# A selective-scan recurrence on four engines: the first half of delta and dx, and the output projection with the residual, moved to other iterations

## What is computed

```
x = resid * rsqrt(mean(resid * resid) + EPS) * norm_w
skip = x @ skip_w.T
x = silu(causal_conv(x @ in_w.T, conv_w, 4 taps) + conv_b)
delta = softplus(x @ Wd1.T @ Wd2_w.T + Wd2_b)
Bm, Cm = x @ WB.T, x @ WC.T
h_l = exp(delta_l * A) * h_(l-1) + (delta_l * x_l) * B_l      # 512 channels x 16 states
y_l = sum over the states of h_l * C_l
y = (y + x * W_D) * silu(skip)
x = layernorm(resid + (resid + y @ out_w.T))
```

## Time and profile before

| | |
|---|---|
| median of 3 runs | 1925.93 us (1924.54 to 1927.51) |
| the profiled execution | 1923.67 us |
| its span, first to last instruction | 1921.8 us |
| busy: PE, DVE, ACT, POOL | 1619.1, 1483.1, 1084.0, 1258.2 us |
| largest group: the scans into ps_h, L690 | 160 x 2287 ns, 24.6 us of waits for ACT |
| mean granted TensorE clock | 0.939 |

### The profile page before, as it was taken

One profiled execution on the slowest core, in us unless ns is written; L12 is line 12 of the kernel. 1 busy time (PEld: TensorE's weight loads), 2 busy tenths in 40 slices (PEclk: granted clock), 3 DMA queues, 4 the chain that ended last, 5 costly groups with the idle time before them and its releaser, 6 DMA issues. The chain is left out here.

```text
span 1921.8 us, 32746 instructions
## 1 busy us (share of the span) xinstructions
PE 1619.1 (84%) x9596; PEld 1040.7 (54%) x9597; DVE 1483.1 (77%) x2444; ACT 1084.0 (56%) x2436; POOL 1258.2 (65%) x936
## 2 busy tenths in 40 slices
PE   7787877778787778874579999898899999999996
PEld 5454444445444444442246666665677555555685
DVE  5799899999999999999868887887633444444488
ACT  4777777788778777875324444444422333333325
POOL 1988888899888889988655788884320333333300
PEclk9889899999999998997679999998999999999999
DMA  7545555444545544446246765443156222222272
GB/s 222 138 102 129 114 133 124 99 106 103 122 110 133 133 111 108 97 106 147 64 117 161 185 184 154 134 138 95 54 170 231 86 85 85 85 86 85 71 268 88
DMA packets 179286, 238.30 MB, mean 124 GB/s; under 512 B 24714, under 2 KB 115725, under 8 KB 177070
## 3 DMA queue, kind: packets, MB, share of 16 engines
q1 hardware_dynamic: 160606, 200.64, 40.8%
q0 software_dynamic: 9888, 27.80, 4.1%
q10 hardware_dynamic: 8656, 8.18, 1.6%
HBM read 172.15 MB, written 65.90 MB: 124 GB/s over the span
## 5 line engine op out<-in xcount | busy, mean ns | idle before, releaser
L690 DVE TENSOR_TENSOR_SCAN ps_h<-ps_h,inject 128x1024 f32<-128x1024 f32 x160 | 365.9, 2287 | 24.6 <-ACT ps_h L534 24.6
L364 POOL TENSOR_TENSOR inject<-common,bc_n 128x2048 f32<-128x2048 f32 x63 | 285.7, 4548 | 86.1 <-issue 72.3
L364 POOL TENSOR_TENSOR inject<-dx_n,bc_n 128x2048 f32<-128x2048 f32 x64 | 290.2, 4547 | 0.0
L1518 ACT ACTIVATE expT<-ps_t 128x512 f32<-128x512 f32 x256 | 148.7, 596 | 199.2 <-PE ps_t L2015 195.2
L534 ACT ACTIVATE ps_h<-delta_n,a_neg 128x256 f32<-128x256 f32 x512 | 213.0, 462 | 61.8 <-DVE hc L703 42.4
L534 ACT ACTIVATE ps_h<-common,a_neg 128x256 f32<-128x256 f32 x512 | 212.0, 463 | 43.0 <-DVE hc L703 33.1
L1646 DVE TENSOR_REDUCE neg_max<-ps_s 128x2 f32<-128x512 f32 x256 | 172.8, 681 | 79.0 <-PE ps_s L2004 74.1
L373 POOL TENSOR_TENSOR h_pool<-h_pool,bc_n 128x1024 f32<-128x1024 f32 x96 | 226.8, 2363 | 0.0
L690 DVE TENSOR_TENSOR_SCAN h_pool<-ps_h,inject 128x1024 f32<-128x1024 f32 x96 | 218.6, 2277 | 5.7 <-ACT ps_h L534 3.0
L2666 PE MATMUL ps_uh<-arena,s_xT 128*128 x440 | 210.3, 601 | 4.9 <-issue 4.9
L2370 POOL DMA_INDIRECT token_results<-common,e_y_row x82 | 80.0, 976 | 188.7 <-DVE common L2519 188.7
(11 more groups left out here) (338 smaller groups left out, 3580.6 us busy)
## 6 DMA issues: line engine op xcount, KB each, us to landing
common<-dup_rows SPq DMA_DIRECT2D x120, 256.0 KB, 6.0
bc_n<-bc_rows SPq DMA_DIRECT2D x64, 256.0 KB, 4.4
delta_n<-dup_rows SPq DMA_DIRECT2D x64, 256.0 KB, 4.4
dx_n<-dup_rows SPq DMA_DIRECT2D x64, 256.0 KB, 7.5
arena<-slot_rows SPq DMA_DIRECT2D x110, 136.0 KB, 2.1
arena<-token_results SPq DMA_DIRECT2D x8, 1536.0 KB, 18.5
dup_rows<-delta SPq DMA_DIRECT2D x32, 256.0 KB, 4.0
dup_rows<-dx SPq DMA_DIRECT2D x32, 256.0 KB, 4.2
```

The lines of the kernel that those rows point to most:

```text
L364: nc.gpsimd.tensor_tensor(inject[:, at:at + 2, :, :], dx_n[c // 2][:, None, :, c % 2, :].to_broadcast([P, 2, JB, L]), bc_n[b % 2][:, 0, nq ...
L690: nc.vector.tensor_tensor_scan(out.rearrange("p j t -> p (j t)"), ps_h[k % 2][:, :, :].rearrange("p j t -> p (j t)"), inject[:, k % RING, ...
L1518: nc.scalar.activation(expT[:, h % (2 * HG), :, :], ps_t[h % 2][:, :, :], ACT.Exp).then_inc(h_exp, 1)
```

## The change

No instruction is added or removed. Four things move.
- ScalarE: the copy of the first half of delta stands ahead of the second half's logarithm in iteration 8, instead of behind it.
- VectorE: the first half of dx is made in iteration 8 instead of 9. Since iteration 8 is one that GpSimd weighs, it stands right behind scan 8.
- TensorE: the output projection is in iteration 2 instead of 3, and ahead of that iteration's sums.
- VectorE: residual and row statistics both stand in iteration 4 (before: 5 and 6), mean in 5 (7), variance in 6 (8). The later row steps stay.

```
@@ ScalarE's loop @@
+                if front and i == 8:
+                    take_delta(b + 1, 0)
                 if front and i in (6, 8):
                     softplus_log(b + 1, (i - 6) // 2)
                 if tail and i == 7:
                     layernorm_root(b - 1)
-                if front and i in (8, 10):
-                    take_delta(b + 1, (i - 8) // 2)
+                if front and i == 10:
+                    take_delta(b + 1, 1)
@@ VectorE @@
-            rows = (residual, row_stats, row_mean, row_var, None, square_root, newton, row_scale, row_shift)
+            rows = {4: (residual, row_stats), 5: (row_mean,), 6: (row_var,), 10: (square_root,), 11: (newton,),
+                    12: (row_scale,), 13: (row_shift,)}
...
-                if b > 0 and 5 <= i < 14 and rows[i - 5] is not None:
-                    rows[i - 5](b - 1)
-                if b < B - 1 and i in (9, 11):
-                    make_dx(b + 1, (i - 9) // 2)
+                if b > 0:
+                    for step in rows.get(i, ()):
+                        step(b - 1)
+                if b < B - 1 and i in (8, 11):
+                    make_dx(b + 1, i // 11)
@@ TensorE's loop @@
+                if tail and i == 2:
+                    project_out(b - 1)
                 sums(b, i)
...
-                if tail and i == 3:
-                    project_out(b - 1)
```

More of the change, by code:

```diff
@@ L811, in _ @@
                 split(q_rows[n], q_parts[n], 18 + 4 * (AHEAD + n), qk.q_split)
-            for step in rows:
-                if step is not None:
+            for steps in rows.values():
+                for step in steps:
                     step(B - 1)
```

## The result

| | before | after |
|---|---|---|
| median | 1925.24 us (4 runs) | 1948.06 us (1945.99 to 1953.10, 4 runs) |
| ratio | | 1.0125, 95% interval 1.0104 to 1.0146 |
| the profiled execution, its span | 1923.67, 1921.8 us | 1948.89, 1947.1 us |
| VectorE's period, dx to dx of the first half, mean of 14 | 55.49 us | 57.02 us |
| start of the phase after the recurrence (the cast to `ident_bf` on VectorE) | 951.80 us | 974.1 us |

The change makes the kernel 22.8 us slower, where I had forecast about 12 us (1938) and a range up to 1944. Of the 25.2 us between the two profiled executions 22.3 lie ahead of the phase that follows the recurrence. The direction and the place (the wait for delta ahead of dx) were as forecast; the size was not, since the wait has a second cause that I had left out.

The account below looks back on a forecast made before the run. VectorE's 55.25 us period was taken as the bound, nearly level with a loop through GpSimd. Batch 0's 1.76 us plus 14 x 0.77 gave 12.5, taken as 12.0: 1938 us, own range 1932 to 1944, 1925 to 1944 with B.

Parts of the forecast that it names:

- Batch 0: First batch, without residual: dx would come at 87.00 and scan 10 at 91.07 against 89.31, +1.76 us.
- The hole of the Silu session: VectorE ahead of scan 5: residual and statistics fill the 1.31 us hole, scan 5 stays, 1.25 us leave the path behind.
- The projection ahead of the sums: TensorE: projection runs 343.9 to 347.6, pushed-back sums are done by about 349.1, before their buffers are wanted, so free.
- dx ahead of scan 9: VectorE idles from scan 8's end to dx, 3.1 us instead of 1.13, with scan 9 queued behind; +0.77 us per batch.
- The loop over GpSimd gets slack: GpSimd restarts sooner after dx, TensorE's 1.49 us wait for it goes, db comes earlier; the loop gets 2.5 us of slack.
- delta copy at + 1.59 = 364.16: ScalarE: the delta copy ends at 364.16, directly after decay 10 at 362.57; dx then follows at 364.77.
- The sum: Whole run: 1.76 + 14 x 0.77 = 12.5 us slower, less 0.8 us of old longer waits, taken as 12.0.
- allowance of 0.4 us per batch: Upper range for an unseen later sum or copy collision, from the smallest margin, a 0.38 us hole; gives 1944 us.
- A: Rival: faster, the GpSimd loop sets the period and its ScalarE part shortens 1.70 us; 14 x 1.70 = 24, 1902 us; 5%.
- B: Rival: no change, ScalarE reaches decay 10 when scan 8 ends, needing 0.9 us saved between weighing 7 and delta; 1926 us; 10%.
- C: Rival: slower still, projection ends after 348.3 and the residual holds the scan; 1.25 us more per batch, 1955.5 us; 10%.
- The two holes that I named: GpSimd: about 4 us ahead of the new batch's injects (5.31 before), and a new hole for scan 9 ahead of injects 14 and 15.

Follow-up runs that it names:

- part 1 alone: Changed kernel with delta copy and dx put back as before, keeping the moved projection, residual and row steps: 1921.25 us, ratio 0.9990 to the kernel before.

## Why the prediction was right and wrong

- *Batch 0.* Right, nearly: from scan 5 to the first dx it is 19.32 instead of 20.86 us, and to scan 10 23.40 instead of 21.47, 1.93 us more where I had 1.76.
- *The hole of the Silu session.* Right: residual and statistics went into it without a wait ahead of them, 1.39 us from start to start of scan 5, and scan 5 did not move. The step from residual to statistics was 0.71 us, as taken from the row of the residual. By the rule of the Trainium skill (VectorE: DVE Perf Modes, "The DRAIN you can't avoid") that the semaphore costs nothing extra, as I had applied it, it would have been 0.59; here the measurement decides.
- *The projection ahead of the sums.* Right that it is free: nobody waited for it or for the sums behind it, and with part 1 alone the kernel is not slower. It isn't free wherever VectorE is sooner: with dx back in 9 the residual waited for it 5 times, 2.1 us in all.
- *dx ahead of scan 9.* Right, and the whole of the loss hangs on it: with dx back in 9 the same kernel is 1.0% faster than before. The wait that I worked out, 3.13 us, and the period, 56.02, are what the kernel shows where TensorE is kept at its full clock (3.12 and 56.01), and within 0.1 us in every third batch of the changed kernel.
- *The loop over GpSimd gets slack.* Right: ScalarE copied db at 357.55, with no wait, ahead of decay 7.
- *The step that failed* is "delta copy at + 1.59 = 364.16", right behind decay 10. The copy also waits for TensorE's sum of softplus (`take_delta` waits for `f_sp`, L501). I costed that sum nowhere. Before, it ended at 363.3 and the copy was due at 366.85, so it had 3.5 us of cover. In the changed kernel, in the batch shown, the copy was due at 370.61 and the sum began at 365.32; at the full clock it would have ended at 369.02, with 1.6 us of cover left. So the copy's move alone would not have made it late. But the change also stretched TensorE's idle time ahead of the sum from 2.1 to 3.9 us, mainly by letting db come sooner (with db sooner and nothing else it is 3.6 us), and the sum ran at the lower clock and took 5.2 to 6.7 us instead of 3.7. Less the cover of 1.6, that is 0 to 1.4 us too late, and the copy waited 0 to 1.5 us. Against the kernel kept at the full clock it is 0.94 us a batch on the mean (57.02 against 56.08), 13.2 us in all.
- *The sum.* From scan 5 of batch 0 to the last scan 10 that stands behind a first-half dx, the profiled execution takes 23.3 us longer than before. My terms give 12.5 us. Of the 3.4 us by which the old batches were longer than 14 x 55.25 all went, where I had taken 0.8 (and 12.5 - 0.8 is 11.7, not the 12.0 that I took). That leaves 9.1; batch 0 adds 0.2, the first period, with the longer scaling of `bq`, 0.8, and the sum of softplus 13.2: together 23.3 us. So the forecast was out by one large term that it didn't have, and the allowance of 0.4 us per batch was far too small for it.
- *What I read past.* The kernel before already had such matmuls at the lower clock (means of 731 to 810 ns in the same three groups, against 592), hidden under that cover.
- *The rivals.* A (faster, 1902) did not come. With dx left in 9 the kernel does get to 1907 us, but not at A's price: its 14 periods are 12.2 us shorter, where A had 14 x 1.70 = 24. B (no change) needed ScalarE to save 0.9 us ahead of the copy; it saved nothing, and no wait ahead of dx was under 3.2 us. C (the projection late) did not occur in the change. My upper end of 0.4 us per batch was taken from a margin among VectorE's and ScalarE's rows, and so could not hold a term from TensorE.
- *GpSimd.* The two holes that I named are there: the restart waits 4.3 us for the DMA on the mean (60.0 us in 14), where I had 4, and the injects wait for a scan of VectorE's 38.8 us in 15, 2.6 us each, where I had put a hole without a size.

## What to carry to other kernels

Move a producer's step sooner by all means, but leave its consumer, on an in-order engine, behind work that is ready: one scan and one weighing in front of dx were the cover for the copy, and giving that cover up cost 3.1 us of wait, where with the cover and the copy sooner it was at most 0.7. When a copy is moved forward, write down every semaphore that it waits for, not only its place in its queue, with the slack of each; the one with the most slack before can be the one that decides after. And cost a TensorE group behind a hole of a few us at both clock levels, above all if the change makes that hole longer.

## What was not expected of the hardware

Adding matmuls made the kernel faster: 1936.4 against 1948.1 us, by keeping TensorE busy in a hole of 3.9 us, of which 1.14 was left. The control without the repeats had 1949.6 us. The hole's length alone doesn't tell how much of the work behind it is slow: behind holes of 3.93, 3.92 and 3.93 us in three successive batches, with the same instructions, the sum took 6.7, 5.2 and 6.2 us, and this went round in the same order of three from the third batch to the last. In the kernel before, holes of 2.09 us had the sum at the full clock in some batches (3.70 us) and partly at the lower in others (5.40 us).
